# Deformable convolution loop: the column half of the next image placed ahead of the row half, the plain result added in the column half, the sums taken off GpSimd

## The reference

```python
def _L2_conv_ref(x, ...):
    out_standard = conv2d(x, conv_w, conv_b, padding=1)
    offset_x = offset_branch(x, offx_dw_w, ...)   # depthwise 3x3, batch norm, relu, 1x1 to 9 offsets
    offset_y = offset_branch(x, offy_dw_w, ...)
    out_x = dsc_axis(x, offset_x, dscx_w, 'x')    # 9 taps, each sampled at column w + offset, linear
    out_y = dsc_axis(x, offset_y, dscy_w, 'y')    # 9 taps, each sampled at row h + offset, linear
    out = jnp.concatenate([out_standard, out_x, out_y], axis=1)
    out = conv2d(out, fus_w, None, padding=0)     # 1x1 over 96 channels
    return jax.nn.relu(batchnorm(out, fus_bn_g, fus_bn_b))
```

## Time and profile before

| | us |
|---|---|
| runs | 4535.45, 4545.91, 4530.43 |
| median | 4535.45 |
| profiled execution, its own time | 4534.85 |
| its span from first to last instruction | 4533.2 |
| busy in it: PE / DVE / ACT / POOL | 3639.5 / 2529.5 / 2648.5 / 2475.7 |
| the step loop of `deformable`: first and last `read_o` | 1981.08, 4247.48 |

### The profile page before, as it was taken

The page is one execution under the profiler, slowest core; times in us unless marked ns, Lnnn a source line. Parts: engine busy times, 40 slices in busy tenths (PEclk is TensorE's granted clock), DMA queues, the critical chain, the costliest instruction groups (busy, mean ns, idle before and its releaser), DMA issues. The chain is left out here.

```text
span 4533.2 us, 143240 instructions
## 1 busy us (share of the span) xinstructions
PE 3639.5 (80%) x59682; PEld 2155.1 (48%) x59682; DVE 2529.5 (56%) x5104; ACT 2648.5 (58%) x2951; POOL 2475.7 (55%) x1851
## 2 busy tenths in 40 slices
PE   6866448533999965569999999999999999999488
PEld 5765445322333332236655555555555555555222
DVE  5302636543333324447776776767777667776455
ACT  5600004332222224469989889898898988988442
POOL 0000210011000003369999999999999999999600
PEclk9955659855999987779999999999999999999799
DMA  3265649998877865531112121122211212111585
GB/s 95 59 132 124 191 104 255 236 332 225 227 218 210 226 199 168 168 72 56 39 53 59 55 60 41 53 57 56 60 39 55 57 54 60 39 57 42 125 213 128
DMA packets 675524, 532.85 MB, mean 118 GB/s; under 512 B 39434, under 2 KB 600714, under 8 KB 667050
## 3 DMA queue, kind: packets, MB, share of 16 engines
q1 hardware_dynamic: 556444, 386.26, 33.4%
q10 hardware_dynamic: 108560, 105.02, 7.5%
q0 software_dynamic: 9984, 33.56, 2.3%
HBM read 338.51 MB, written 186.19 MB: 116 GB/s over the span
## 5 line engine op out<-in xcount | busy, mean ns | idle before, releaser
L1576 POOL TENSOR_SCALAR df_t<-df_t 128x1536 f32<-128x1536 f32 x1536 | 2225.2, 1806 | 51.2 <-ACT df_t L1614 51.0
L1791 PE MATMUL df_o<-df_t,df_zs 128*32 128x128 f32 x36864 | 1326.2, 277 | 121.1 <-POOL df_t L1576 87.9
L1659 DVE TENSOR_SCALAR df_t<-df_d 128x512 int32<-128x512 int32 x1536 | 1062.3, 692 | 551.8 <-PE df_d L1745 548.8
L1614 ACT ACTIVATE df_t<-df_a 128x1024 f32<-128x1024 f32 x1024 | 1051.4, 1027 | 241.7 <-PE df_a L1745 238.5
L1791 PEld LDWEIGHTS df_o<-df_t,df_zs 128*32 128x32 f32 x36864 | 916.1, 110 | 568.3 <-POOL df_t L1576 265.3
L1745 PE MATMUL df_d<-df_ix,net_sel 11*128 11x512 bf16 x1536 | 593.1, 386 | 1.0 <-DVE df_t L1659 0.9
L1614 ACT ACTIVATE df_t<-df_z 128x1024 f32<-128x1024 f32 x512 | 525.2, 1026 | 60.9 <-PE df_z L1745 24.7
L1618 ACT ACTIVATE df_zs<-df_z 128x864 f32<-128x864 f32 x512 | 453.2, 885 | 2.0 <-PE df_z L1770 2.0
L1745 PE MATMUL df_a<-df_ix,net_sel 11*128 11x512 bf16 x2048 | 398.8, 386 | 37.5 <-DMA df_ix<-offset 37.4
L1770 PE MATMUL df_z<-net_Z,df_x 32*128 32x288 f32 x4096 | 392.8, 427 | 17.9 <-ACT df_x L1631 9.9
L1093 POOL CAST of_parts<-of_t_o 128x512 bf16<-128x512 f32 x64 | 40.1, 626 | 646.4 <-ACT of_t_o L1063 646.4
(11 more groups left out here) (228 smaller groups left out, 4731.5 us busy)
## 6 DMA issues: line engine op xcount, KB each, us to landing
gc_x<-x SPq DMA_DIRECT2D x240, 128.0 KB, 4.8
dc_x<-x SPq DMA_DIRECT2D x240, 128.0 KB, 3.2
dc_xt<-x_2t SPq DMA_DIRECT2D x240, 128.0 KB, 4.6
fw_x<-in_x SPq DMA_DIRECT2D x32, 512.0 KB, 6.8
iv_x<-in_x SPq DMA_DIRECT2D x64, 256.0 KB, 4.7
x<-iv_x POOLq DMA_DIRECT2D x64, 256.0 KB, 4.9
y<-gc_o ACTq DMA_DIRECT2D x64, 256.0 KB, 5.8
r_y<-y SPq DMA_DIRECT2D x8, 2048.0 KB, 14.2
```

Source lines behind the costliest of these rows:

```text
L1576: g.tensor_scalar(t, t, 1.0, 0.0, ALU.min, ALU.max).then_inc(hat_p, 1)
L1614: act.activation(T[:, m % 2, 3 * i:3 * i + 2], src, ACT.Abs).then_inc(a_read, 1)
L1659: v.tensor_scalar(T[:, m % 2, 3 * i + 2].bitcast(I32), ps_d[:].bitcast(I32), 0x7fffffff, None, ALU.bitwise_and).then_inc(d_read, 1)
L1791: mm = pe.matmul(ps_o[32 * q:32 * q + 32, 0:P], Zs[:, m % 2, q, 32 * k:32 * k + 32], T[:, m % 2, 3 * i + x, P * q:P * q + P], start=(k == ...
```

## The change

The 16 halves are put in the order of the list `phases`: column 0, column 1, row 0, column 2, row 1, and so on to column 7, row 6, row 7. A column half's turned result is written and read back during the half behind it, and lands in U before the row half of the same image begins. The row half adds it where it added the plain result before. The plain convolution is computed from the transposed image, so that its result is in the layout of the column half; SP loads it into a new buffer UT, and the column half's `read_o` adds it. `finish`, its semaphores and YR are gone; `stats` and `send` follow the row half's own steps.

```diff
-        kinds = ((X, "LX", "bx"), (X, "LP", "bp"), (XT, "LY", "by"))
+        kinds = ((X, "LX", "bx"), (XT, "LP", "bp"), (XT, "LY", "by"))
...
-        YB, YR = s.sb("yb", [P, C * W]), s.sb("yr", [P, LINES * W])
+        YB, UT = s.sb("yb", [P, C * W]), s.sb("ut", [P, LINES, W])
...
+        phases = [(0, 0)] + [(b + 1 - a, a) for b in range(B - 1) for a in range(2)] + [(B - 1, 1)]
+        ST = LINES * len(phases)
...
+                def phase(t):
+                    b, a = phases[t]
+                    before = phases[t - 1] if t else (None, None)
                     for m in range(1, LINES + 1):
+                        spread_past(LINES * t + m)
+                        if t + 1 < len(phases) and m <= 8:
+                            if m == 1 and t:
+                                sp.wait_ge(z_full, LINES * t)
                             for p in (2 * m - 2, 2 * m - 1):
+                                load_image(t + 1, p)
+                        if before[1] == 0:
+                            bt = before[0]
+                            if m == 1 and bt > 1:
+                                sp.wait_ge(u_out, 16 * NCH * (bt - 1))
+                                sp.wait_ge(counted, NCH * (bt - 1))
+                            if m == 5:
+                                sp.wait_ge(kept, LINES * (bt + 1))
+                            if 5 <= m < 13:
+                                put_turned(bt, m - 5)
+                            if m == 17:
+                                sp.wait_ge(uy_out, 128 * (bt + 1))
+                            if 17 <= m and m % 2 and (m - 17) // 2 < 8:
+                                get_turned(bt, (m - 17) // 2)
+                        c, r = divmod(m - 8, 4)
+                        if r == 0 and c >= 0:
+                            if a == 1:
+                                send(t, b, c)
+                            elif b + 1 < B:
+                                sp.wait_ge(o_read, LINES * t + SC * (c + 1) + 1)
+                                load_plain(b + 1, c)
+                        if t + 1 < len(phases) and m % SI == 0:
+                            load_offsets(t + 1, m // SI - 1)
+                    if a == 1:
+                        send(t, b, NCH - 1)
+                    elif b + 1 < B:
+                        sp.wait_ge(o_read, LINES * (t + 1) + 1)
+                        load_plain(b + 1, NCH - 1)
...
-                for p in range(16):
-                    load_image(0, 1, p)
-                images_in_turn(image)
                 for c in range(NCH):
-                    send(B - 1, (B - 1) % 2, c)
+                    load_plain(0, c)
+                for t in range(len(phases)):
+                    phase(t)
...
-                def finish(b, par, c):
-                    r = slice(SC * c * W, SC * (c + 1) * W)
-                    if c == 0:
-                        g.wait_ge(uy_in, 128 * (b + 1))
-                    g.wait_ge(o_read, ST * b + LINES + SC * (c + 1) + 1)
-                    ur = U[:, par].rearrange("p j w -> p (j w)")[:, r]
-                    g.tensor_tensor(ur, ur, YR[:, r], ALU.add).then_inc(summed, 1)
...
-                        v.tensor_scalar(XO[:, m % 2], ps_o[:, 0:P], S[:, 0, j:j + 1], None, ALU.add).then_inc(o_read, 1)
+                        if j % (LINES // 2) == 0:
+                            v.wait_ge(ut_in[2 * j // LINES], 8 * NCH * (b + 1))
+                        v.scalar_tensor_tensor(out=XO[:, n % 2], in0=ps_o[:, 0:P], scalar=S[:, t % 2, j:j + 1], in1=UT[:, j],
+                                               op0=ALU.add, op1=ALU.add).then_inc(o_read, 1)
...
+                    c, r = divmod(j - 5, SC)
+                    if r == 0 and c >= 0 and phases[t][1] == 1:
+                        stats(t, c)
+                    if j == 1 and t and phases[t - 1][1] == 1:
+                        stats(t - 1, NCH - 1)
+                stats(len(phases) - 1, NCH - 1)
...
-        cw[:, p, :, p:p + 3] = c("conv_w").transpose(0, 3, 2, 1)
+        cw[:, p, :, p:p + 3] = c("conv_w").transpose(0, 2, 3, 1)
```

More of the change, by code:

```diff
@@ L1462, in deformable, with phase_of, turned_rows @@
         ixv = IX[:].rearrange("r (q p) -> r q p", q=4)
[L1464 to L1469, removed]
+        def phase_of(n):
+            return phases[n // LINES] if 0 <= n < ST else (None, None)
+        def turned_rows(b):
+            return U[:, 1].rearrange("p j w -> p (j w)") if b == 0 else YB[:]
         with s.block() as block:
@@ L1523, in image @@
[L1523 to L1554, removed]
@@ L1632, in normalise @@
                                    scale=GS[:, 1, b:b + 1]).then_inc(xn, 1)
-                def image(b, par, more):
-                    for m in range(ST):
-                        a, j = divmod(m, LINES)
-                        if more or m + 2 < ST:
-                            ahead_of(*ahead(b, m, 2))
-                        if 10 <= j < 18 and (more or a == 0):
-                            normalise(*((b, 1) if a == 0 else (b + 1, 0)), j - 10)
                 for i in range(3):
-                    distances(0, 0, i)
@@ L1644, in _ @@
-                normalise(0, 0, 0)
-                read_z(0, 0)
-                ahead_of(0, 1)
+                    distances(0, i)
+                normalise(0, 0)
+                read_z(0)
+                ahead_of(1)
                 for p in range(1, 8):
-                    normalise(0, 0, p)
-                images_in_turn(image)
+                    normalise(0, p)
+                for n in range(ST):
+                    t, j = divmod(n, LINES)
+                    if n + 2 < ST:
+                        ahead_of(n + 2)
+                    if 10 <= j < 18 and t + 1 < len(phases):
+                        normalise(t + 1, j - 10)
@@ new lines, in _ @@
+                for p in range(8):
+                    line_sums(0, p)
+                read_s(0)
+                for n in range(ST):
+                    t, j = divmod(n, LINES)
+                    more = t + 1 < len(phases)
+                    if n + 2 < ST:
+                        near(n + 2, 0)
+                    if j == TJ and more:
+                        read_s(t + 1)
+                    if n + 2 < ST:
+                        near(n + 2, 1)
+                    if phase_of(n - 1)[1] == 0:
+                        keep(n - 1)
+                    read_o(n)
+                    if n + 2 < ST:
+                        near(n + 2, 2)
+                        read_z(n + 2)
+                    if 18 <= j < 26 and more:
+                        line_sums(t + 1, j - 18)
+                    c, r = divmod(j - 5, SC)
[3 more added lines that the diff above has]
+                        stats(t - 1, NCH - 1)
@@ L1818, in _ @@
                 pe.wait_ge(lined, 48)
[L1819 removed]
+                for n in range(2):
                     for i in range(3):
[L1821 to L1822 removed]
+                        spreads(n, i)
+                    if n == 0:
                         pe.wait_ge(xn, 1)
[L1824 removed]
+                    make_z(n)
                 pe.wait_ge(zd_read, 3)
[L1826 removed]
+                line_totals(0)
```

286 lines of the change are left out of this document (110 added, 176 removed).

## The result

| | before | after |
|---|---|---|
| median of the runs, us | 4532.94 (4 runs) | 4453.65 (4 runs) |
| profiled execution, its own time | 4534.85 | 4453.85 |
| its span | 4533.2 | 4452.2 |
| first to last read of ps_o in the loop | 2266.4 | 2189.6 |
| last read to the next stage | 5.2 | 2.8 |

The ratio is 0.9822, with a 95% interval of 0.9808 to 0.9837: 79 us faster, by the interval 74 to 87. The prediction said 4456 and 79.2 us; the 4456 went from the median of three runs of the kernel before, 4535.45, which the fourth run lowered by 2.5. The granted clock was 1.00 through the loop in both kernels, so the clock plays no part in this difference.

What follows compares the result with a forecast made beforehand. The prediction took POOL, always full in this stage while others wait, as the bound. Additions leaving POOL 76.8 us plus the stage's end 2.4 gave 79.2 us saved, so a median of 4456 us, range 4446 to 4472.

Steps and rivals of the forecast that it cites:

- POOL is the bound, by starts and not by records: Loop: each addition leaving POOL saves its 1.25 us between starts, not its record's length; 76.8 us in all.
- The end of the stage: After the loop's last read: the last piece no longer waits for POOL's last sums and statistics; 2.4 us saved.
- `depth_conv` itself, whose term I put at 0: Plain convolution stage: another tile feeds the same number of multiplications of the same shape; cost 0.
- The new read and the moved statistics at no cost: DVE: column read with UT stays at 351 ns; statistics moved to row halves are covered by POOL's work; cost 0.
- The rival with contention: Column halves: DVE's new read, with an SBUF operand, is held while POOL works; 4612 us, chance 0.03.
- POOL still the bound in column halves: Column halves: the others keep up with POOL's 137.3 us a half; priced 0, upper end 1.6 us.
- a dip of 1.6 covered by 3.3: Column halves: the others lose 1.6 us in steps with `normalise`; the 3.3 us lead from row halves covers it.
- every half would be near 137.3: Sign of being right: every half from the fourth on takes near 137.3 us, by starts of reads.
- The second rival: Column halves: the other engines bind, no backlog carries over, 24 us given back; 4480 us, chance 0.08.
- the main case: Whole kernel: POOL stays full; 4456 us, own range 4449 to 4465, chance 0.85.
- SP's queue: SP: 52 issues in a row half's phase, where 44 were the most before, delay no needed load; cost 0.

Runs made afterwards that it cites:

- 1: Changed kernel with 64 additions of 128x512 put back on POOL, on scratch tensors nothing reads, 8 in each column half: 4534.0 us, ratio 0.9999.
- 2: Kernel before, old order of halves, with POOL's additions of the turned result left out, so the output lacks it: 4458.2 us, ratio 0.9828.
- 3: Changed kernel with the column half's read as before, without the UT operand, so the output lacks the plain result: 4458.3 us, ratio 0.9835.
- 5: Kernel before, old order of halves, with the 64 additions of the turned result on DVE instead of POOL, same output: 4601.3 us, ratio 1.0141.
- experiment 6: Changed kernel with 64 more DVE tensor_scalar instructions of 128x512 on unused data: reading SBUF 4559.0 us, reading PSUM 4451.6 us.
- 7: Changed kernel with more ACT activations of 128x512 in each of six column halves: with 8, 4450.6 us; with 16, 4480.2 us.

## Why the prediction was right

*POOL is the bound, by starts and not by records.* Shown by 1 and 2: the gain can be put back and taken away with nothing but POOL's instructions. The loop from first to last read lost 2266.40 - 2189.58 = 76.8 us, the term was 76.8. The mechanism is right and the term is good to about half a us; that it came out to the tenth, and the whole to 79.3 against 79.2 where the runs give 74 to 87, is luck.

*The end of the stage.* 5.17 to 2.83 is 2.34 us, the term was 2.4. The two make 79.2 of the 81.0 us between the profiled executions; the other 1.8 lie outside this stage: the loop began 2.5 us earlier, all of which was there before `depth_conv` began, and the closing took 0.6 longer. `depth_conv` itself, whose term I put at 0, took 552.3 us before and 552.6 after.

*The new read and the moved statistics at no cost.* Shown by 3, and by the 351 ns. The rival with contention was rightly given a low chance, for this operand and not for its kind: 5 shows that the additions with both inputs in SBUF, 64 of 128x512, cost 2.2 us each and turn the gain into a loss. The prediction cited the page too widely: with at most one SBUF input an instruction is free of this only outside the modes with two ports, and the `tensor_scalar` of experiment 6 has one SBUF input and was held.

*POOL still the bound in column halves.* Right, with a size that was guessed. I had steps of 4.19 us regained after a dip of 1.6 covered by 3.3. The trace shows the dip: the steps with `normalise` are the others' pace, not POOL's, so a column half takes 137.9 by its reads and the row half 136.6, and only their pair keeps POOL's time; by the starts of the hats each half takes 137.3. My statement that every half would be near 137.3 was off by 0.6 each way. The margin, shown by 7, is more than 8 and less than 16 activations a half. By the time from a hat's inputs being ready to its start, the backlog falls to 2.6 us in the changed kernel's column halves from column 2 on, and in experiment 2, where the statistics lie in them too, from 1.8 us in column 1 to 1.0 in column 7; the total is the same. The second rival was nearer than the main case let see.

*SP's queue.* No wait of a half for a load showed; POOL's 0.5 us of idle time leaves no room for one. What the order covers was not in my sum, and my later price of it, 8 to 12 us an image, was about half of the 22.4 measured.

## What to carry to other kernels

When an engine is full and others wait for it, an instruction taken off it is worth its distance between starts, whatever the utilisation of the rest; check only that a slower stretch of the others fits into its backlog. Where an addition is to move to VectorE beside a busy GpSimd, look at its form: here it was free as part of an instruction that reads PSUM anyway, and cost 2.2 us with two inputs in SBUF. And a result that must go through DRAM needs other work between the way out and its use, so the order of the halves and the place of the addition belong together.

## What the runs showed that I had not expected

A DVE instruction of a form that contends is not always held for one GpSimd instruction only. It can lose the next turns too, until GpSimd pauses: up to 6.8 us for an addition that takes 0.67 alone. It can also get in between two hats and make GpSimd wait, 38 of 64 times in experiment 5 and 24 of 64 in experiment 6. The 8 long holds all began with three hats ready; but in experiment 6 one hat was ready in nearly all cases, short and long, so what decides between one turn and the next stays open. Behind such holds PE stood still and then ran at the lower clock for some 126 us, so the length of the records is not the whole price.

And a plane of work moved to DVE, which was busy 103 of 137 us in a column half, cost 155 us even in PSUM: by the waits, free time on an engine was of no use inside the chain that runs through it. Whether it is outside of that chain no run here tried.
